# A four-layer graph network with residual layer norms on one core: the inputs of layers 1 and 2 turned by DMA transposes, with new order lists

## The reference

```
x = _layernorm(x + _L0_gnn_ref(...))   # two hypergraph convolutions, ReLU and layer norm between them, 256 -> 512 -> 256
x = _layernorm(x + _L1_gnn_ref(...))   # w_i = q_i . sum_j adj_ij k_j;  softmax(w)_i * v_i
x = _layernorm(x + _L2_gnn_ref(...))   # 8-head attention, scores * (2 adj), projections with biases
x = _layernorm(x + _L3_gnn_ref(...))   # tanh-gated input, QK^T * adj, rows divided by their sums, two projections, ReLU
```

## Time and profile before

| | |
|---|---|
| median of 3 runs | 927.14 us (926.74 to 928.84) |
| the profiled execution | 925.54 us, of which the span of instructions is 923.5 us |
| granted TensorE clock, mean | 0.992 |
| busy in the span | PE 94%, DVE 83%, ACT 77%, POOL 70% |
| DMA engines | 50% of the time of all 16 |
| chain that ended last | PE 61%, DVE 16%, DMA 7%, SP's queue 6%, issue 5%, ACT 4% |

### The profile page before, as it was taken

How to read it: one execution, slowest core, us unless ns; L and a number is a source line. 1 busy time by engine, 2 the same in 40 slices (tenths; PEclk the granted TensorE clock), 3 DMA queues, 4 the chain that set the end, 5 groups by cost and what they waited for, 6 DMA issues and landing times.

```text
span 923.5 us, 34918 instructions
## 1 busy us (share of the span) xinstructions
PE 872.6 (94%) x12412; PEld 751.6 (81%) x12412; DVE 764.8 (83%) x2387; ACT 714.8 (77%) x1772; POOL 650.3 (70%) x973
## 2 busy tenths in 40 slices
PE   7788899999999999999999999999999999988884
PEld 6677778888888888888888888888888888876774
DVE  5657888889888898988889899988889888987642
ACT  3466678888898888888888888888888898876542
POOL 3556667877778777887777877778877778763321
PEclk9999999999999999999999999999999999999998
DMA  7003455655455655555545555545555455566531
GB/s 222 25 23 102 123 129 132 138 131 134 133 135 147 153 142 132 142 152 128 134 131 133 136 154 147 143 131 149 140 128 136 130 138 143 137 133 133 122 72 35
DMA packets 239634, 118.41 MB, mean 128 GB/s; under 512 B 145634, under 2 KB 239332, under 8 KB 239588
## 3 DMA queue, kind: packets, MB, share of 16 engines
q1 hardware_dynamic: 239588, 117.80, 50.4%
HBM read 50.38 MB, written 25.17 MB: 82 GB/s over the span
## 4 chain that ended last, share of the span: by engine, by line
PE 61%; DVE 16%; DMA 7%; SPq 6%; issue 5%; ACT 4%; POOL 1%; ACTq 0%; DVEq 0%; POOLq 0%
PE bank L545 15%; PE bank L547 13%; PE bank L546 13%; PE bank L586 3%; PE bank L775 3%; PE bank L828 3%; DMA k_by_head<-kst 2%; PE bank L759 2%; DVE preC L1283 2%; DVE z1l L1060 2%; DMA Ks<-k_by_head 2%; PE bank L702 2%; SPq L393 2%; DVE vst L1060 2%; SPq L417 1%
## 5 line engine op out<-in xcount | busy, mean ns | idle before, releaser
L1420 POOL TENSOR_TENSOR rFl<-r,rFh 128x512 f16<-128x512 f32 x64 | 73.0, 1159 | 14.9 <-ACT rFh L855 14.7
L1521 POOL TENSOR_TENSOR late<-late,Smx 128x512 f32<-128x512 f32 x64 | 67.1, 1049 | 11.2 <-DVE Smx L1319 10.0
L545 PE MATMUL bank<-z1h,W 128*128 128x256 f16 x256 | 70.1, 274 | 4.0 <-DVE z1l L1060 1.3
L545 PE MATMUL bank<-W,rFh 128*128 128x256 f16 x256 | 70.8, 277 | 1.7 <-DVE W L1060 1.7
L547 PE MATMUL bank<-W,rFl 128*128 128x256 f16 x256 | 70.6, 276 | 0.0
L546 PE MATMUL bank<-W,rFh 128*128 128x256 f16 x256 | 70.5, 276 | 0.0
L546 PE MATMUL bank<-z1l,W 128*128 128x256 f16 x256 | 69.8, 273 | 0.0
L547 PE MATMUL bank<-z1h,W 128*128 128x256 f16 x256 | 69.8, 273 | 0.0
L886 ACT ACTIVATE late<-preG,nbG,rsG 128x256 f32<-128x256 f32 x64 | 35.0, 593 | 44.5 <-POOL nbG L1442 44.5
L1428 POOL TENSOR_SCALAR veC<-sqC 128x2 f32<-128x2 f32 x32 | 6.1, 191 | 77.4 <-ACT x L875 77.2
L915 ACT ACTIVATE r<-bank,b1c 128x256 f32<-128x256 f32 x128 | 52.7, 463 | 5.3 <-PE bank L547 5.2
(11 more groups left out here) (279 smaller groups left out, 4130.7 us busy)
## 6 DMA issues: line engine op xcount, KB each, us to landing
Qs<-q_by_head SPq DMA_DIRECT2D x96, 128.0 KB, 2.6
Ks<-k_by_head SPq DMA_DIRECT2D x96, 128.0 KB, 2.5
Vbd<-vst SPq DMA_DIRECT2D x128, 66.0 KB, 2.1
xin<-x SPq DMA_DIRECT2D x32, 256.0 KB, 2.9
q_by_head<-qst SPq DMA_DIRECT2D x32, 256.0 KB, 2.3
k_by_head<-kst SPq DMA_DIRECT2D x32, 256.0 KB, 2.2
out<-late SPq DMA_DIRECT2D x32, 256.0 KB, 2.2
aC<-adj_mask SPq DMA_DIRECT2D x32, 129.0 KB, 2.1
```

Source lines behind the costliest of these rows:

```text
L545: pe.matmul(o, sh, mh, start=start, stop=False, skip_group_check=True)
L1420: return pool.tensor_tensor(dst, a, b, ALU.subtract)
L1521: pool.tensor_tensor(Ssb[:, t], Sm[:, t], Smx[:, t:t + 1].rearrange("p t h -> p h t").broadcast_to([P, HEADS, NODES]), ALU.subtract).then_ ...
```

## The change

- PE: the two `turn`s (eight float32 transposes per group) are gone. `Gm`, `uxT` and `Wv1` read `x1T`, `Wq`, `Wk` and `Wv` read `x2T` (`project_turned`, `project_rows`).
- SP: two new DMA transposes per group, `turn_x1` and `turn_x2`, each [128, 1024] float16. `x1T` is double-buffered, `x1s`, `x2s` and `x2T` are not.
- ACT: the high halves are cast from x1 in SBUF and from x2 in PSUM, not turned, into `x1s` and `x2s`. The norm "C" writes x2 to the PSUM bank bD0 (the score bank of tile 0), and first waits until the last group's scores in it were read (`s_masked`). The squares go to a scratch tile.
- POOL: makes the low half of x1 from SBUF; the addition of the bias (`x2b`) is gone from it.
- DVE: `x1Fl` is gone, `x2s`'s low half takes the place of `x2Fl`, and `x2b` is now DVE's, read from bD0. `Wk` overwrites bD0, so PE waits for it (`x2_biased`).
- All order lists, and the places and numbers of the bursts: 46 in the fill (41 before) and 43 in the drain (43 before).

```diff
-ORDER_PE = [1, 3, 2, 3, 2, 4, 4, 0, 2, 1, 5, 0, 2, 0, 5, 0, 3, 5, 3, 1, 0, 5, 4, 2, 5, 5, 1, 2, 0, 1, 0]
+ORDER_PE = [1, 4, 2, 3, 2, 3, 5, 2, 1, 0, 5, 4, 0, 2, 0, 5, 3, 3, 0, 5, 0, 5, 5, 4, 1, 2, 0, 1, 0]
...
+            def turn_x2(at):
+                sp.wait_ge(ev("x2_lo"), at.n()).then_inc(ev("sp_held"), 1)
+                if at.earlier(1):
+                    sp.wait_ge(ev("v"), at.n(-1)).then_inc(ev("sp_held"), 1)
+                sp.dma_start_transpose(x2T[:].rearrange("p t l c k -> p (t l c) k"),
+                                       x2s[:].rearrange("p t l d -> p (t l d)")).then_inc(ev("x2_turned"), 16)
...
-                pe.wait_ge(ev("xB"), at.n())
                 if at.earlier(1):
                     pe.wait_ge(ev("preC"), at.n(-1))
-                turn(bC, x1[:, at.par]).then_inc(ev("x1_turned"), 1)
-                yield
-                pe.wait_ge(ev("x1F_lo"), at.n())
-                project_fm(bC, Gm, x1Fh[at.par], x1Fl[at.par]).then_inc(ev("u"), 1)
+                pe.wait_ge(ev("x1_turned"), at.chain(16, 16))
+                project_turned(bC, Gm, x1T[at.par]).then_inc(ev("u"), 1)
...
-                pe.wait_ge(ev("x2F_lo"), at.n())
-                project_fm(bD1, Wq, x2Fh, x2Fl).then_inc(ev("q"), 1)
+                pe.wait_ge(ev("x2_turned"), at.chain(16, 16))
+                project_turned(bD1, Wq, x2T).then_inc(ev("q"), 1)
                 yield
 
             def stream3(at):
                 first_needs(at, 6)
-                project_fm(bD0, Wk, x2Fh, x2Fl).then_inc(ev("k"), 1)
+                pe.wait_ge(ev("x2_biased"), at.n())
+                project_turned(bD0, Wk, x2T).then_inc(ev("k"), 1)
...
-                squares_of("C", x2, at)
-                yield
-                norm("C", x2, at)
-                yield
-                act.wait_ge(ev("x2_turned"), at.n())
-                cast(x2Fh[:].rearrange("p c k -> p (c k)"), bD0[:]).then_inc(ev("x2F_hi"), 1)
+                squares_of("C", sqscr, at)
+                yield
+                if at.earlier(1):
+                    act.wait_ge(ev("s_masked"), at.tile(0, -1))
+                norm("C", bD0[:].rearrange("p (t d) -> p t d", t=TILES), at)
+                yield
+                act.wait_ge(ev("xC"), at.n())
+                if at.earlier(1):
+                    act.wait_ge(ev("x2_turned"), at.chain(16, 16, -1))
+                cast(x2s[:, :, 0], bD0[:].rearrange("p (t d) -> p t d", t=TILES)).then_inc(ev("x2_hi"), 1)
...
             def stream3(at):
+                if at.earlier(2):
+                    dve.wait_ge(ev("preF"), at.n(-2))
+                if not at.earlier(1):
+                    dve.wait_ge(ev("unstaged"), 8)
+                dve.wait_ge(ev("xC"), at.n())
+                dve.tensor_tensor(x2b[:, at.par], bD0[:].rearrange("p (t d) -> p t d", t=TILES),
+                                  bob[:].rearrange("p (o d) -> p o d", o=1).broadcast_to([P, TILES, D]), ALU.add
+                                  ).then_inc(ev("x2_biased"), 1)
...
+                pool.wait_ge(ev("x1_hi"), at.n())
+                sub(x1s[:, :, 1], x1[:, at.par], x1s[:, :, 0]).then_inc(ev("x1_lo"), 1)
```

More of the change, by code:

```diff
@@ L194, in build @@
         am = sb("am", [P, TILES, NODES])
-        x1Fh = [sb(f"x1Fh{i}", [P, 2, TOK], F16) for i in range(2)]
-        x1Fl = [sb(f"x1Fl{i}", [P, 2, TOK], F16) for i in range(2)]
+        x1s = sb("x1s", [P, TILES, 2, D], F16)
+        x1T = [sb(f"x1T{i}", [P, TILES, 2, 2, P], F16) for i in range(2)]
         uh = sb("uh", [P, 2, TOK], F16)
@@ L211, in build @@
         acD = sb("acD", [P, 2, TILES, NODES])
-        x2Fh = sb("x2Fh", [P, 2, TOK], F16)
-        x2Fl = sb("x2Fl", [P, 2, TOK], F16)
+        x2s = sb("x2s", [P, TILES, 2, D], F16)
+        x2T = sb("x2T", [P, TILES, 2, 2, P], F16)
         qst = sb("qst", [P, 2, 2, TOK], F16)
@@ L698, in stream1 @@
                     for k in range(2):
-                        for i, (uu, xx) in enumerate(((uh, x1Fh[at.par]), (uh, x1Fl[at.par]), (ul, x1Fh[at.par]))):
+                        for i, (uu, hl) in enumerate(((uh, 0), (uh, 1), (ul, 0))):
                             for b in range(2):
@@ L702, in stream1 @@
                                 m = pe.matmul(bC[64 * b:64 * b + 64, t * NODES:(t + 1) * NODES], uu[:, k, tok],
-                                              xx[:, k, tok], start=(k == 0 and i == 0), stop=(k == 1 and i == 2),
+                                              x1T[at.par][:, t, hl, k, 64 * b:64 * b + 64], start=(k == 0 and i == 0), stop=(k == 1 and i == 2),
                                               skip_group_check=True)
@@ L940, in stream1 @@
                 yield
-                act.wait_ge(ev("x1_turned"), at.n())
-                cast(x1Fh[at.par][:].rearrange("p c k -> p (c k)"), bC[:]).then_inc(ev("x1F_hi"), 1)
+                act.wait_ge(ev("xB"), at.n())
+                if at.earlier(1):
+                    act.wait_ge(ev("x1_turned"), at.chain(16, 16, -1))
+                cast(x1s[:, :, 0], x1[:, at.par]).then_inc(ev("x1_hi"), 1)
                 yield
@@ L1238, in stream1 @@
                 yield
-                dve.wait_ge(ev("x1F_hi"), at.n())
-                low(x1Fl[at.par][:].rearrange("p c k -> p (c k)"), bC[:],
-                    x1Fh[at.par][:].rearrange("p c k -> p (c k)")).then_inc(ev("x1F_lo"), 1)
-                yield
                 dve.wait_ge(ev("u_hi"), at.n())
@@ L1509, in stream3 @@
             def stream3(at):
-                if at.earlier(2):
-                    pool.wait_ge(ev("preF"), at.n(-2))
-                if not at.earlier(1):
-                    pool.wait_ge(ev("unstaged"), 8)
-                pool.wait_ge(ev("xC"), at.n())
-                bias_tm(x2b[:, at.par], x2[:], bob).then_inc(ev("x2_biased"), 1)
-                yield
                 for t in range(TILES):
```

58 lines of the change are left out of this document (31 added, 27 removed).

## The result

The changed kernel takes **939.18 us** in the median of four runs (936.13 to 944.09), the kernel before 926.94 on the same chip (922.47 to 928.84): a ratio of 1.0144, 95% interval 1.0087 to 1.0202. The forecast was 939.6. The profiled execution is the slowest of the four, 944.09 us with a span of 942.3; the other spans are 934.3 to 938.3.

The account below looks back on a forecast made before the run. A closed loop of waits through DVE was to replace PE as the bound, step 25.8 us against 25.58. From 925.5, +6.5 for steps and +6 for fill and drain gave 938, 939.6 with 1.6 to the median; range 911 to 956.

Parts of the forecast that it names:

- PE's turns gone, 24.65 us if PE stayed the bound: On PE, dropping the transposes of x1 and x2 saves 0.93 us a step, giving 24.65 us if PE stayed the bound.
- The rival that PE stays the bound: DVE's sums are too long by over 1 us and the step falls towards 24.65: 909 us; chance 0.22.
- Part 1, c to W1a, 6.48 us: From conv2's end on PE (c) to W1a: 6.48 us through DVE's chain; W1a waits 0.9 to 1.2 us for z1l.
- Part 2, 9.15: From W1a to the end of Wq on PE: 9.15 us.
- Part 3, 5.2: From Wq through ACT and DVE to Wk: 5.2 us; Wk waits 0.4 us for x2b.
- Part 4, 5.0: From the start of Wk to the end of conv2 on PE: 5.0 us.
- SP, "being in no chain that I see for longer than that": SP issues two more transposes a step at 1.25 us each, which it can do; so far no cost.
- The transposes, some 0.7 us to spare: In full steps cxT, x1T and x2T land before PE needs them, each some 0.7 us to spare, costed at nothing.
- The contention rival: cxT, x1T and x2T in a row slow each other and Gm waits each step: 947 to 961 us; chance 0.12.
- Fill and drain, +6: Outside the full steps, the longer way of x1 and x2 costs 0 to 12.4 us; half taken, +6 us.
- The step's lower value of 25.5: Sum of the loop's four parts with the lower value at each place: 25.5 us, against 25.8 forecast.
- the DMA rival: Transposes landing over 0.7 us late on busy DMA engines add 8 to 21 us to 938: 947 to 961; chance 0.12.

Follow-up runs that it names:

- e6: Changed kernel with SP loading acD behind the first PT transpose and DVE making kst's low half ahead of HBl: 956.51 us, ratio 1.0313.
- e9: Changed kernel with SP loading acD ahead of cxT, where SP is idle: 941.84 us, ratio 1.0196 to the kernel before.
- e12: e9 with DVE's Ql one column wide of 256 in the full steps: 939.09 us, ratio 1.0163 to the kernel before.
- e10: Changed kernel with DVE's x2b one column wide instead of 256 per tile in the full steps: 942.86 us, ratio 1.0212.
- e8: Kernel before, with two more DMA transposes of cxs behind each cxT into tiles that nobody reads: 928.86 us, ratio 1.0059.
- e11: Changed kernel with POOL making x1's low half one column wide in the full steps: 940.07 us, ratio 1.0174.
- e2: Changed kernel with DVE making z1l ahead of deg and SA, and ACT z1h ahead of the second cxs: 949.77 us, ratio 1.0235.
- e4: Changed kernel with x1's low half made by DVE instead of POOL in the full steps: 951.89 us, ratio 1.0253.

## Why the prediction was right

- *PE's turns gone, 24.65 us if PE stayed the bound.* The turns are gone, PE's share fell to 95.8% (I had said 95 to 96), and the step did not follow. The rival that PE stays the bound is refuted. By PE's busy time a step lost 0.6 us (25.38 to 24.79, the share in the windows times the step), not the 0.93 of the prediction; what makes the difference was not looked for.
- *Part 1, c to W1a, 6.48 us.* 6.44 where it was read, and preB to z1l 5.15 against 5.19. Shown by e6 and e9: when k's way is shortened, W1a waits for z1l and c to W1a stays. But the account by waits was wrong: 25 to 30 us at W1a were forecast, 1.1 in the full steps came, and 17.6 stood at the scores, for Ks. In every second step Ks held W1a up to 0.3 us longer than z1l did, so the mean of c to W1a is 6.56. The typical step is 25.73 to 25.9 us; the mean of 25.88 has two of 26.8 at its start. DVE's chain is also not DVE's alone: e12 shows ACT's way from Dinv to Ph to be as long.
- *Part 2, 9.15.* 9.14.
- *Part 3, 5.2.* 5.27, though not for the reason given alone. The ACT and DVE chain to x2b has the predicted length, and beside it the sums wait 0.28 us for POOL's rsq, which I did not have; e10 shows that this second path holds Wk where it is without x2b.
- *Part 4, 5.0.* 4.90.
- *SP, "being in no chain that I see for longer than that".* This step was wrong. SP stood between kst and Ks, the park's distance from kst's low half went from 0.1 to 0.8 us, and k's way became as long as DVE's. It cost little (e9: 0.02 us a step) because other chains were as late.
- *The transposes, some 0.7 us to spare.* cxT, x1T and x2T were issued 1.5, 2.9 and 4.3 us behind W1a (1.4, 2.7, 4.0 forecast) and landed after 3.3, 3.4 and 3.1 us in the median; PE waited for x1T and x2T 4.3 us in the whole run. The contention rival is refuted by this, and by e8. But of the 0.7 us to spare little is left: in the step shown x1T lands, by the median, at 6.3 us behind W1a, and Gm starts at 6.52. The prediction had also weighed an estimate of 10.5 us for eight blocks, from the 1309 ns for one block of the Trainium skill's page "VectorE: DVE Perf Modes", section "The three transpose paths". The trace doesn't agree: eight blocks landed after 3.1 to 3.4 us.
- *Fill and drain, +6.* About 5 by the medians, some 4 at equal granted clock. The first full step came 5.8 (by conv2) to 7.7 us (by cxT) later, not 2 to 5, in the slowest of four executions; what of it is the longer way of x1 and x2, what SP's load and what the clock was not separated. The half of 12.4 us was a choice, not a sum.
- *The bounds.* The step's lower value of 25.5 does not follow from the parts: with 4.9 for part 4 they give 25.7, with PE's 4.8 in part 3 as well 25.3. The times of the DMA rival, 947 to 961, are counted from 939.6, not from the 938 written there.

The time was right to 0.4 us, with steps of +7.5 for +6.5 and fill and drain of 5 for 6, two misses that cancel. Such closeness is luck; what was sound is the sum along the loop, right to 0.1 us in each part where it was read. Two waits were named, and in the runs at least four chains tied.

## What to carry to other kernels

In an order fitted as closely as this one, several chains can end within 0.1 us of each other at a meeting point. A sum along one closed loop gave the length of the step well, but the row of waits will name whichever chain is last by a hair, and to shorten only that one gives nothing (e9, e10, e11, e12) or costs (e2, e4, e6). Count the queue that issues the DMAs as an engine of the loop, and read what stands ahead of an issue, not only whether the queue has time left over. Before moving a DVE instruction by half a microsecond, look at what POOL does at the new place (e6).

## What the runs showed of the hardware

DVE operations with two inputs in SBUF and POOL operations slowed each other here, by up to 0.7 us. HBl beside POOL's y0l took 1.34 us and 0.62 without it (e6). DVE's x2s, which reads one of its inputs from PSUM, took 0.68 us (456.10, changed kernel) in the midst of two POOL subtractions (455.45 to 457.49), no more than the same kind of operation elsewhere (y3l, 0.68). In the changed kernel Ehl now meets POOL's two rsq additions. POOL's timeline:

```profile
460.00 1.27 POOL L1493 TENSOR_TENSOR rsq<-rsq 128x512 f32<-128x512 f32 x1
461.36 1.06 POOL L1496 TENSOR_TENSOR rsq<-rsq 128x256 f32<-128x256 f32 x1
```

And DVE's timeline in the same stretch of the changed kernel:

```profile
460.64 1.18 DVE L1343 TENSOR_TENSOR Ehl<-E,Ehl 128x512 f16<-128x512 f32 x1
```

Ehl takes 1.18 us there, and 0.68 later in the same step (465.28), where POOL has only an operation on 128x2 elements beside it; the second rsq takes 1.06 (also the median of the run), and took 0.73 in every step before. These 0.33 us are as long as the sums' wait of 0.28. That this overlap causes that wait is read from the trace and was not tried by a run of its own. In e4 Ehl started when the first rsq was nearly over, took 0.71, and the second rsq again 1.06. The Trainium skill, "SBUF — State Buffer", section "SBUF: two separate sides", says that the two engines share a pair of ports under an exclusive lock, held for a whole instruction, and that a DVE operation with two SBUF inputs falls under it against a GpSimd operation that reads SBUF. These rows agree in the main: the one that starts first runs at its own pace, and the other grows by 0.33, 0.50 and 0.72 us, where 0.46, 0.63 and 0.93 us of the first were left (the second rsq, Ehl, HBl).
